# A mixed block in float32: the last layer's rounding constant on VectorE, its output added by POOL, its scale worked out in every partition

## The reference

```
def quant_fp8(x):
    amax = max(abs(x))                                  # over the whole tensor
    scale = minimum(448 / maximum(amax, 1e-12), 448)
    return clip(x * scale, -448, 448).astype(float8_e4m3fn), 1 / scale

w_fp8, w_scale = quant_fp8(weight)                      # 256 x 256
x_fp8, x_scale = quant_fp8(layernorm(x))
out = ((x_fp8 @ w_fp8.T) * (x_scale * w_scale) + bias).astype(bfloat16)
x = x + out
```

## Time and profile before

| | |
|---|---|
| median of 3 runs | 927.66 us |
| the runs | 919.22, 927.66, 927.92 us |
| span of the profiled execution | 920.5 us |
| time of that execution beside its span | the page gives none |
| the last layer's loop | from 878.75 us, ScalarE's first scaling, to the end |
| last rounded half of the last block | 912.73 us |
| last addition to `x` | 917.68 us |

### The profile page before, as it was taken

The page is one execution under the profiler, slowest core; times in us unless marked ns, Lnnn a source line. Parts: engine busy times, 40 slices in busy tenths (PEclk is TensorE's granted clock), DMA queues, the critical chain, the costliest instruction groups (busy, mean ns, idle before and its releaser), DMA issues.

```text
span 920.5 us, 18650 instructions
## 1 busy us (share of the span) xinstructions
PE 854.3 (93%) x5904; PEld 782.6 (85%) x5904; DVE 726.2 (79%) x1821; ACT 526.9 (57%) x1454; POOL 365.6 (40%) x412
## 2 busy tenths in 40 slices
PE   6899999999999999999979999999899999999535
PEld 6889999999999998898968999999688888888424
DVE  7788788978878978788756667778746889878988
ACT  5776566656765755454524445445455566665377
POOL 3234334424333424766640310241665757431330
PEclk9999999999999999999999999999989999999858
DMA  9999990000100003343224433544311111000004
GB/s 307 309 315 332 316 294 1 0 0 0 35 0 0 2 1 98 104 127 126 98 75 115 142 106 126 151 133 128 109 56 43 53 36 47 24 1 2 0 23 160
DMA packets 51771, 91.89 MB, mean 100 GB/s; under 512 B 5381, under 2 KB 26298, under 8 KB 51697
## 3 DMA queue, kind: packets, MB, share of 16 engines
q1 hardware_dynamic: 45105, 72.87, 25.0%
q0 software_dynamic: 6592, 18.07, 6.4%
HBM read 34.56 MB, written 56.36 MB: 99 GB/s over the span
## 4 chain that ended last, share of the span: by engine, by line
PE 42%; DVE 8%; DMA 3%; POOL 3%; issue 3%; ACT 2%; SPq 1%; DVEq 0%; POOLq 0%; ACTq 0%
PE acc L2128 7%; PE py L1231 7%; PE score L2112 4%; PE py L1167 3%; PE pg L1167 3%; PE proj L2061 3%; DMA xn<-dispatched 2%; PE acc L1180 2%; PE proj L2080 2%; POOL dispatched L1676 2%; PE tr L1224 2%; PE tr L2023 1%; DVE routed L2786 1%; PE pgate L1268 1%; PE acc L2090 1%
## 5 line engine op out<-in xcount | busy, mean ns | idle before, releaser
L535 POOL TENSOR_TENSOR prob<-prob,row_inv 128x462 f32<-128x462 f32 (+1 forms) x96 | 83.8, 875 | 178.6 <-DVE row_inv L711 178.6
L898 PE MATMUL acc<-u,probT 128*128 128x256 f32 (+1 forms) x960 | 134.1, 289 | 1.0 <-DVE u L723 1.0
L595 ACT ACTIVATE prob<-score,neg_max 128x77 f32<-128x77 f32 x512 | 121.3, 353 | 13.3 <-DVE neg_max L705 13.0
L851 PE MATMUL score<-m,xnT 128*128 128x462 f32 (+1 forms) x576 | 122.6, 350 | 0.0
L898 PEld LDWEIGHTS acc<-u,probT 128*128 128x128 f32 (+1 forms) x960 | 119.4, 189 | 1.9 <-DVE u L723 1.4
L851 PEld LDWEIGHTS score<-m,xnT 128*128 128x128 f32 x576 | 96.2, 188 | 5.7
L1231 PE MATMUL py<-w1T,hidT 128*128 x426 | 93.1, 354 | 0.0
L2128 PEld LDWEIGHTS acc<-vz,prob 128*128 128x128 f32 (+1 forms) x640 | 78.8, 196 | 13.8 <-issue 12.2
L585 ACT ACTIVATE probT<-tr 128x512 fp32r<-128x512 f32 (+1 forms) x96 | 52.1, 545 | 66.0 <-PE tr L837 65.6
L1676 POOL DMA_INDIRECT dispatched<-xn,slots x64 | 69.7, 1090 | 43.8 <-DVEq L1460 26.6
L2128 PE MATMUL acc<-vz,prob 128*128 128x34 f32 (+2 forms) x640 | 80.8, 280 | 1.2 <-DVE vz L2325 1.2
(11 more groups left out here) (381 smaller groups left out, 2088.3 us busy)
## 6 DMA issues: line engine op xcount, KB each, us to landing
dispatched<-zeros SPq DMA_DIRECT2D x1, 33664.0 KB, 111.0
xn<-dispatched SPq DMA_DIRECT2D x71, 128.0 KB, 2.1
dispatched<-hid SPq DMA_DIRECT2D x71, 128.0 KB, 1.7
out<-x_res SPq DMA_DIRECT2D x7, 512.0 KB, 2.6
x_res<-in_x SPq DMA_DIRECT2D x1, 3072.0 KB, 16.0
consts<-in_L_ffn_W SPq DMA_DIRECT2D x8, 384.0 KB, 3.3
consts<-in_L_ffn_Ws SPq DMA_DIRECT2D x3, 384.0 KB, 3.9
x_res<-in_x SPq DMA_DIRECT2D x2, 512.0 KB, 9.0
```

The costliest lines, as they stand in the source:

```text
L535: gp.tensor_tensor(pr, pr, row_inv[t % 2][:, heads(k)].unsqueeze(2).to_broadcast([P, BANK_HEADS[k], KEYS]), ALU.mult).then_inc(prob_ready, 1)
L595: last = act.activation(prob[t % 2][:, h * KEYS:(h + 1) * KEYS], score_of(t, k)[:, n * KEYS:(n + 1) * KEYS], ACT.Exp, bias=neg_max[t % 2][ ...
L851: last = pe.matmul(score_of(t, k)[:, 0:BANK_HEADS[k] * KEYS], xnT[blk][i][:, dc, j * P:(j + 1) * P], m[w][:, dc, cols(k)], start=(n == 0 a ...
L898: last = pe.matmul(acc[t % 2][:, 0:D], probT[t % 2][i][0:rows, c, :], u[k][0:rows, c, :], start=(c == 0 and q == 0), stop=(c == KCH - 1 an ...
```

## The change

- The rounding constant: ScalarE's `round_at` goes. VectorE makes it with one scalar operation, `max(e, 2**-6) * ROUND_AT`; the two steps behind it are then a plain addition and a plain subtraction. VectorE's order is addition of block `n`, constant of `n + 1`, subtraction of `n`, mask of `n + 2`. The memset of `floor` goes.
- The output: POOL adds blocks 0 to 6 to `x`, behind its bias steps; VectorE adds the last block in its halves, counted by a semaphore of its own, `x_last`, for which SP waits after the seven stores.
- The scale: the maxima are turned spread over 128 columns, so that the row of all 128 maxima stands in every partition; each partition reduces it and works out the scale itself. The turn back, the row's copy and the copy of the pair go. The clamp at 1e-12 is a further column of `xf_max`, set by POOL. ScalarE and POOL start when `scales[:, 0:1]` is there; the second reciprocal and `dequant` come after.
- ScalarE issues its four first scalings without anything between them.

```diff
-        amax, limit = sb("x_amax", [P, 1], F32), sb("x_limit", [1, 2], F32)
-        scales, dequant, floor = sb("scales", [P, 2], F32), sb("dequant", [P, 1], F32), sb("floor", [P, 1], F32)
+        amax, limit = sb("x_amax", [P, 1], F32), sb("x_limit", [P, 1], F32)
+        scales, dequant = sb("scales", [P, 2], F32), sb("dequant", [P, 1], F32)
...
@@ sync
-                    sp.wait_ge(fs["x_out"], LAST + 1 + a)
+                    sp.wait_ge(fs["x_last"], a + 1)
@@ gpsimd
+                gp.memset(g["xf_max"][:, NBLK + 1:], AMAX_MIN).then_inc(fs["rows_set"], 1)
...
-                gp.wait_ge(fs["limit_done"], 7)
+                gp.wait_ge(fs["limit_done"], 3)
...
+                for n in range(LAST):
+                    gp.wait_ge(fs["z_out"], 2 * n + 2)
+                    xb = g["x"][:, n, :, :].rearrange("p j d -> p (j d)")
+                    gp.tensor_tensor(xb, xb, z[n % 2], ALU.add).then_inc(fs["x_out"], 1)
@@ scalar
-                def round_at(n):
-                    act.wait_ge(fs["e_ready"], n + 1)
-                    act.activation(e[n % E_BUFS], e[n % E_BUFS], ACT.Relu, scale=ROUND_AT, bias=floor[:, 0:1]).then_inc(fs["m_ready"], 1)
...
-                act.wait_ge(fs["limit_done"], 7)
-                scaled(0)
-                scaled(1)
-                round_at(0)
-                round_at(1)
-                scaled(2)
-                scaled(3)
-                act.wait_ge(fs["limit_done"], 8)
+                act.wait_ge(fs["limit_done"], 3)
+                for n in range(V_BUFS):
+                    scaled(n)
+                act.wait_ge(fs["limit_done"], 5)
                 for n in range(LAST):
                     copy_qT(n)
-                    if n + 2 < NBLK:
-                        round_at(n + 2)
@@ vector
-                dve.memset(floor[:, :], -ROUND_AT * FP8_MIN_NORMAL)
...
+                dve.wait_ge(fs["rows_set"], 3)
                 dve.tensor_reduce(amax[:, 0:1], g["xf_max"][:, :], AX_X, ALU.max).then_inc(s["max_out"], 1)
                 dve.wait_ge(fs["small_mm"], 1)
-                ffn_scales(dve, limit, scale_row, small[0:1, 0:P], fs["limit_done"])
-                dve.wait_ge(fs["small_mm"], 2)
-                dve.tensor_copy(scales[:, :], small[:, P:P + 2]).then_inc(fs["limit_done"], 1)
-                dve.wait_ge(fs["limit_done"], 7)
+                dve.tensor_reduce(limit[:, 0:1], small[:, 0:P], AX_X, ALU.max).then_inc(fs["limit_done"], 1)
+                dve.wait_ge(fs["limit_done"], 1)
+                dve.reciprocal(limit[:, 0:1], limit[:, 0:1]).then_inc(fs["limit_done"], 1)
+                dve.wait_ge(fs["limit_done"], 2)
+                dve.tensor_scalar(scales[:, 0:1], limit[:, 0:1], FP8_MAX, FP8_MAX, ALU.mult, ALU.min).then_inc(fs["limit_done"], 1)
+                dve.wait_ge(fs["limit_done"], 3)
+                dve.reciprocal(scales[:, 1:2], scales[:, 0:1]).then_inc(fs["limit_done"], 1)
...
+                def round_at(n):
+                    dve.wait_ge(fs["e_ready"], 2 * n + 1)
+                    dve.tensor_scalar(e[n % E_BUFS], e[n % E_BUFS], FP8_MIN_NORMAL, ROUND_AT, ALU.max, ALU.mult).then_inc(fs["e_ready"], 1)
+
+                def shifted(n, at):
+                    dve.wait_ge(fs["e_ready"], 2 * n + 2)
+                    dve.tensor_tensor(v[n % V_BUFS][:, at], e[n % E_BUFS][:, at], v[n % V_BUFS][:, at], ALU.add).then_inc(fs["t_done"], 1)
+
+                def rounded(n, at, count):
+                    dve.wait_ge(fs["t_done"], count)
                     if n >= 2:
                         dve.wait_ge(fs["tr_mm"], n - 1)
+                    dve.tensor_tensor(q16[n % 2][:, at], e[n % E_BUFS][:, at], v[n % V_BUFS][:, at], ALU.subtract).then_inc(fs["q_ready"], 1)
...
                 power(0)
+                round_at(0)
                 power(1)
-                for n in range(NBLK + 2):
-                    if n < NBLK:
-                        rounded(n)
+                for n in range(LAST):
+                    shifted(n, slice(0, DC * TB))
+                    round_at(n + 1)
+                    rounded(n, slice(0, DC * TB), n + 1)
                     if n + 2 < NBLK:
                         power(n + 2)
-                    if n >= 2:
-                        add(n - 2)
+                halves = [slice(2 * a * D, 2 * (a + 1) * D) for a in range(2)]
+                for a in range(2):
+                    shifted(LAST, halves[a])
+                for a in range(2):
+                    rounded(LAST, halves[a], LAST + 1 + a)
+                xb = g["x"][:, LAST, :, :].rearrange("p j d -> p (j d)")
+                for a in range(2):
+                    dve.wait_ge(fs["z_out"], 2 * LAST + a + 1)
+                    dve.tensor_tensor(xb[:, halves[a]], xb[:, halves[a]], z[LAST % 2][:, halves[a]], ALU.add).then_inc(fs["x_last"], 1)
@@ tensor
-                ffn_transpose_amax(pe, g, small, amax, fs["small_mm"])
-                pe.wait_ge(fs["limit_done"], 6)
-                ffn_spread_scales(pe, g, small, scale_row, fs["small_mm"])
+                pe.transpose(small[:, 0:P], amax[:, 0:1].to_broadcast([P, P]), g["ident"][:, :]).then_inc(fs["small_mm"], 1)
```

More of the change, by code:

```diff
@@ L1948, in attention1 @@
         ffn_bias, ident16 = sb("ffn_bias", [1, D], F32), sb("ffn_ident", [P, P], BF16)
-        amax, limit = sb("x_amax", [P, 1], F32), sb("x_limit", [1, 2], F32)
-        scales, dequant, floor = sb("scales", [P, 2], F32), sb("dequant", [P, 1], F32), sb("floor", [P, 1], F32)
+        amax, limit = sb("x_amax", [P, 1], F32), sb("x_limit", [P, 1], F32)
+        scales, dequant = sb("scales", [P, 2], F32), sb("dequant", [P, 1], F32)
         flat = lambda tile: tile[:, :, :].rearrange("p j d -> p (j d)")
         quarter = lambda m: flat(y)[0:1, m * D:(m + 1) * D]
-        bias_part, scale_row = quarter(0), quarter(1).rearrange("o (i p) -> o i p", p=P)
+        bias_part = quarter(0)
         bias_piece = [flat(y)[0:1, 2 * D + m * P:2 * D + (m + 1) * P].bitcast(BF16) for m in range(len(BIAS_AT))]
@@ L1961, in attention1 @@
         ffn_acc, small = [score[0], score[1], acc[2], acc[3]], tr
-        ffn_names = ("bias_in", "small_mm", "limit_done", "v_ready", "e_ready", "m_ready", "t_done", "q_ready",
-                     "tr_mm", "qT_out", "mm", "z_out", "x_out", "stored", "ident_out", "rows_set", "part_step")
+        ffn_names = ("bias_in", "small_mm", "limit_done", "v_ready", "e_ready", "t_done", "q_ready",
+                     "tr_mm", "qT_out", "mm", "z_out", "x_out", "x_last", "stored", "ident_out", "rows_set", "part_step")
         fs = {n: ctx.enter_context(nc.semaphore(n + "4")) for n in ffn_names}
@@ L2773, in power @@
                     dve.tensor_scalar(e[n % E_BUFS].bitcast(I32), v[n % V_BUFS].bitcast(I32), EXPONENT_BITS, None, ALU.bitwise_and).then_inc(fs["e_ready"], 1)
-                def rounded(n):
-                    dve.wait_ge(fs["m_ready"], n + 1)
-                    if n == LAST:
-                        dve.wait_ge(fs["tr_mm"], n - 1)
-                        for a in range(2):
-                            at = slice(2 * a * D, 2 * (a + 1) * D)
-                            vh, eh = v[n % V_BUFS][:, at], e[n % E_BUFS][:, at]
-                            dve.scalar_tensor_tensor(vh, eh, ROUND_AT * FP8_MIN_NORMAL, vh, ALU.add, ALU.add).then_inc(fs["t_done"], 1)
-                            dve.wait_ge(fs["t_done"], n + 1 + a)
-                            dve.scalar_tensor_tensor(q16[n % 2][:, at], eh, ROUND_AT * FP8_MIN_NORMAL, vh, ALU.add, ALU.subtract).then_inc(fs["q_ready"], 1)
-                        return
-                    dve.scalar_tensor_tensor(v[n % V_BUFS], e[n % E_BUFS], ROUND_AT * FP8_MIN_NORMAL, v[n % V_BUFS], ALU.add, ALU.add).then_inc(fs["t_done"], 1)
-                    dve.wait_ge(fs["t_done"], n + 1)
+                def round_at(n):
+                    dve.wait_ge(fs["e_ready"], 2 * n + 1)
+                    dve.tensor_scalar(e[n % E_BUFS], e[n % E_BUFS], FP8_MIN_NORMAL, ROUND_AT, ALU.max, ALU.mult).then_inc(fs["e_ready"], 1)
@@ L2788, in rounded @@
+                def shifted(n, at):
[3 more added lines that the diff above has]
+                    dve.wait_ge(fs["t_done"], count)
                     if n >= 2:
                         dve.wait_ge(fs["tr_mm"], n - 1)
-                    dve.scalar_tensor_tensor(q16[n % 2], e[n % E_BUFS], ROUND_AT * FP8_MIN_NORMAL, v[n % V_BUFS],
-                                             ALU.add, ALU.subtract).then_inc(fs["q_ready"], 1)
@@ L2793, in add @@
-                def add(n):
-                    parts = (slice(0, TB * DC),) if n < LAST else [slice(2 * a * D, 2 * (a + 1) * D) for a in range(2)]
-                    for a, at in enumerate(parts):
-                        dve.wait_ge(fs["z_out"], 2 * n + a + (2 if n < LAST else 1))
-                        xb = g["x"][:, n, :, :].rearrange("p j d -> p (j d)")[:, at]
-                        dve.tensor_tensor(xb, xb, z[n % 2][:, at], ALU.add).then_inc(fs["x_out"], 1)
```

(3 more changed lines are left out.)

1 line of the change is left out of this document (added).

## The result

The change made the kernel slower. The median is 942.33 us (938.87, 939.84, 944.82, 946.22) against 923.82 us before (919.22, 919.98, 927.66, 927.92); the ratio is 1.0164 with an interval of 1.0108 to 1.0221, so that it is slower by 1% and more, while 2% is neither shown nor excluded. The forecast of 936.7 us (0.97% more) had the side right and the main cost, the shared port; the time lies 1.3 us above its range. So they are compared by ratios to the kernel before on the same chip, and by one stretch of their profiles. The changed kernel was measured on two of these chips again, with ratios of 1.0111 and 1.0127.

A forecast was written before the change was run, and what follows sets the result against it. VectorE and ScalarE were full; after, one port bounds: 878.8 + 28.3 + 1.4 + 15.3 = 923.8, then 1.7 idle, last halves and 2.85 give span 929.5, 9.0 longer. Time 927.66 + 9.0 = 936.7 us, range 927 to 941.

The forecast's parts named there:

- The scale chain: Ahead of the last layer's loop: ScalarE starts 0.67 us plus a 0.15 us allowance earlier in the chain, gaining 1.15 us.
- VectorE alone: Last layer's loop: with the memory to itself, VectorE needs 28.3 us to the last rounded half, 3.5 us a block.
- The port: Last layer's loop: VectorE and POOL share one memory port, so seven POOL additions cost VectorE 7 x 2.18 = 15.3 us.
- POOL's hold: Each POOL addition in the loop holds the memory port for 2.39 less 0.13 = 2.26 us.
- the time when neither engine has anything to do: Near the end, before the last finishes, VectorE and POOL idle between 0.2 and 2.1 us, taken as 1.7.
- The check of the sum on before: The same accounting on the kernel before gives 912.7 for the last half's end; the trace has 912.73, trusted within a us.
- At each instruction's end the other engine gets its turn: In the last layer VectorE and POOL alternate at the port, one instruction each; no size of its own.
- An addition was to be through at most 1.1 + 2.3 us after its finish: In the loop, POOL's addition ends that soon after ScalarE's finish, within the 5.7 us of a block.
- Rival (b): In the loop POOL gets no turn until VectorE runs dry; idle time added, span 931 to 933, time 938 to 940; chance 0.10.
- from the last addition to the end it is 920.5 - 917.68 = 2.85 us: At the program's end: the time behind the last addition stays 2.85 us, as in the kernel before.

The follow-up runs named there:

- the runs with and without starvation: The change unaltered: ratio to before 1.0111, stretch 56.3 us; the change with each block's subtraction right behind its addition: 1.0106, 56.4 us.
- the three kernels without the computation: Against the kernel before, the computation is left out: x is copied to the output, then VectorE streams run with POOL additions; one addition alone takes 2.12 us.
- the loop of ten blocks: Computation left out; VectorE runs ten blocks in the changed kernel's order, POOL's addition allowed after a varied block: 24 to 25.3 us after block 3.

## Why the prediction was right and wrong

**The scale chain** was right: ScalarE starts 1.44 us behind x_amax's start in place of 2.60, a gain of 1.16 against 1.15. The first mask comes 1.18 us behind it, as taken.

**VectorE alone** was right: the block without POOL is 3.48 us (3.5).

**The port** was right in kind. The Trainium skill, SBUF — State Buffer, section "SBUF: two separate sides", has the lock exclusive and held for a whole instruction. The runs agree: POOL's addition, 2.12 us alone, takes 3.03 beside VectorE's additions, and a mask of 0.69 takes 2.35 beside POOL's. In before's time (5.52 us taken off) POOL's seventh addition ends at 924.95 (925.5 in the forecast) and VectorE's last half at 926.1 (926.7). Within the sum, POOL's hold was taken 0.27 us too long for each of seven additions, 1.9 us in all, since the 16-bit operand makes the addition 2.12 us. Working against it, the time when neither engine has anything to do before the last finishes is 2.05 us, from the last half's end at 924.20 to 926.25, where I took 1.7. Some 1.0 us more went into single waits that I haven't followed. So the end of the additions came out within 0.6 us by errors that cancel. The check of the sum on before doesn't bear it out closely either: the terms named there, from the first mask at 879.93, give 912.4 and not 912.7, though still within the us that was claimed (912.73).

**"At each instruction's end the other engine gets its turn"** was wrong as a rule. It holds only while VectorE has issued fewer than some five instructions without a gap; in the earlier trace rows VectorE is held up by POOL or ScalarE every instruction or two, so no such stream stands there, and I made a rule for one from them. An addition was to be through at most 1.1 + 2.3 us after its finish; the first took 11.43 us in each of the five profiles with VectorE's changed order and POOL's additions. Rival (b) had the pattern but not the price: the runs with and without starvation end alike. Its 1.5 to 3.5 us of idle time on top did not show in the end; POOL held the port during VectorE's idle time.

**The step that failed** is "from the last addition to the end it is 920.5 - 917.68 = 2.85 us". It was 6.28 us. I took the constant from a kernel in which POOL had stopped 33 us before the end, and didn't ask what the engine that now works last needs to close. The row that would have told it was there: POOL's drain of 8.5 us at 886.1. Two runs with opposite edits show it: POOL stopping earlier gives 3.6 to 3.8 us of stretch back with the last addition where it was, and an idle memset late ends the program 3.6 us behind the stores. Of the 3.4 us that this step was short, some 3.0 are POOL's drain outlasting the stores. The other 0.4 lie between the last addition and the stores' end, which varies by as much (2.6 to 3.2 us in the profiles here). Together with +8.4 us up to the last addition this gives the 11.9 us of the stretch, where 9.0 was forecast.

**The rest of the time**, 5.5 of 17.4 us of the profile, lies ahead of x_amax, where no timed work was edited. On the other chips the change is 1.1 to 1.3% slower, close to 11.9 us (1.3%), as if that part were chance. The profiles don't settle it: on one chip x_amax came at 889.3 to 894.2 us in three kernels with the old rounding and at 899.8 and 904.3 in two with the new, on another at 891.1 and 892.1 in two with the new. Why TensorE's clock was low for some 14 us more in the untouched layers is open; the forecast gave it no room upward.

## What to carry to other kernels

Moving work to an idle engine buys nothing if both engines go through one port to the memory: add up what both hold it, as on one engine, before counting an idle engine as free. When an edit makes an engine work later than before, look up that engine's closing drain in the profile of the kernel at hand, since its length differs from program to program; here two additions kept on VectorE gave back 3.6 to 3.8 of 11.9 us. And judge an edit that touches one stretch by that stretch, cut at an instruction that both kernels have: it repeated within 0.2 us for the changed kernels, where ratios moved by 1%. Take more than one profile of the kernel before as well; here its stretch could be off by 0.6 us.

## What the runs showed of the hardware

POOL's drain at the end of the program ended 7.2 us behind POOL's last instruction in all kernels with the whole computation, from 887.40 to 894.60 before, from 930.47 to 937.68 after, and as long behind a memset of 0.10 us (933.94 to 941.2). That isn't so for every drain of POOL. An earlier part of the program closes with one as well (L520), and it ends with POOL's last instruction:

```profile
336.51 1.67 POOL L535 TENSOR_TENSOR prob<-prob,row_inv 128x462 f32<-128x462 f32 x2 [0.82 <-DVE row_inv L711]
...
L520 POOLq DRAIN  x1: 812/812/812, 337.4 to 337.4; - x1
```

In the three kernels without the computation it ends at most 0.1 us behind POOL's last addition (158.56 + 3.10 = 161.66 against 161.7 in the first of them). All these stand ahead of, or do without, the transfers that POOL issues itself from 359.9 us on (DMA_INDIRECT, L1676 and L2514), and the long ones behind them. Whether those transfers are the cause, no run told apart. Nor was it tried to leave POOL's closing drain out, as the program does for another of its parts (`nc.Block(no_gpsimd_drain=True)`, L1698).

VectorE shuts POOL out for as long as it streams, up to 24 to 25.3 us in the loop of ten blocks, once it has issued between four and six instructions without a gap. That held for additions of 1024 and 512 columns and for additions mixed with scalar operations, and one wait of VectorE lets POOL in. POOL's addition of 128x1024 is 2.12 us with a 16-bit second operand and 2.39 to 2.40 with two of 32 bits.
